# Three 32 KB-row buffers in place of four 16 KB-row buffers, and a pipeline of four stages in place of five, in a graph attention kernel

## The chip, the cores and the metric

The kernel runs on one core of one Trainium2 chip. The metric is the device time of one execution in microseconds; three executions of the kernel before took 718.99, 719.43 and 722.22 us, with a median of 719.43 us. The core has a matrix engine (PE, whose weight loads are listed as PEld), a vector engine (DVE), a scalar engine (ACT), a general engine (POOL) and a queue engine (SP) that issues transfers. Sixteen DMA engines carry the transfers of all queues.

## The reference

One layer of graph attention over 8192 nodes with 128 features, a residual sum and a layer norm:

```python
h = x @ W
e = (h @ a1)[:, None] + (h @ a2)[None, :]
e = where(e > 0, e, 0.2 * e)
e = where(adj > 0, e, NEG)          # adj: 8192 x 8192 int32, 1 with probability 0.000244
out = layernorm(x + elu(softmax(e, axis=1) @ h))
```

The adjacency matrix is 268.4 MB and holds about two ones in a row. A row without any has equal weights on all 8192 nodes, which gives the mean of x.

## The kernel before

The matrix is read once, and the few ones of each row are found on the way. 128 rows are a *tile* (64 tiles); a tile is loaded in two *halves* of 4096 columns (128 partitions by 16 KB, 2 MB). Two tiles are a *group*, so there are 32 groups, with four halves (quarters q = 0 to 3 of `step`) in each. Each half is used twice:

- PE *folds* it (`fold_half`, L649 and L653): nine products sum eight slices of 512 columns, weighted by powers of two, into one PSUM bank, so that a number in the bank tells in which columns of the half the ones stand. DVE takes the eight largest numbers of each row (`pick`, MAX8).
- ACT squares it and sums it (`square_half`, L551), only to count the ones; the count is compared at the end with what was found, and rows in which they differ (none here) would be computed again.

A group's further work runs in stages, one step of the loop later for each. In the step that folds group n, the functions with p1 work on group n-1, p2 on n-2, and so on:

- `lists` (DVE, at the end of a group's own step) turns the picked numbers into column codes and counts them.
- p1: `count_starts` (PE) sums the counts over the rows, `route` (DVE) and `fill_edges` (PE) bring the ones of a group into one list of 640 edges, `indices` (DVE) makes row numbers of x, `gather` (POOL) fetches these rows of x with five indirect DMAs, and `edges_to_rows` and `mark_empty` (POOL) build masks.
- p2: `neighbour_scores` (DVE), `send_scores` (PE), `scores` (DVE), `exp_weights` (ACT), `weights` (DVE), `send_shares` (PE), `edge_weights` (DVE), `spread_weights` (POOL).
- p3: `sum_neighbours` (PE), `copy_sums` (ACT), `times_W` (PE), `exp_elu` (ACT).
- p4: `finish` (DVE: the sum with x, and the statistics of the norm) and `norm_factors` (POOL); p5: `scale` (ACT).

Every engine runs its own list, written by hand in its `step`, in the order in which the calls stand. Engines wait for one another by counting semaphores. What sets the pace of the loads is `adj_sb` with LOAD_SLOTS = 4 places of one half: SP waits until the half that lay in a place is squared and folded, and then issues the next load into it. All loads, those of x (four, behind the first four halves) and the stores of the result stand in SP's one queue; the gathers go through POOL's queue, and W and a through ACT's.

The first six steps are written out, the middle ones are a loop with two steps in its body, and the last two and what is left of the last groups (the *tail*, from the landing of the last half on) are written out again. In the tail, five matrix products in a row and the like (`keep_warm`) do no work. SP stores groups 0 to 11 and 12 to 23 of the result in one transfer each as soon as it has issued the last load, and the others as they are ready.

## Time and profile before

| | |
|---|---|
| median of three runs | 719.43 us |
| profiled execution | 721.3 us |
| its span, first to last instruction | 719.5 us |
| granted PE clock, mean | 0.882 |
| busy: PE, DVE, ACT, POOL | 557.4, 480.7, 520.5, 443.6 us |
| DMA packets, bytes | 34582, 285.57 MB |

The profiled execution took 1.8 us more than its span (721.3 against 719.5 us). The views are: the page, whose strips cut the span in 40 slices of 18 us; the table by stretches, with the busy time of each engine, the granted clock (1.00 is 2.4 GHz, 0.50 is 1.2 GHz), the DMA engines' mean busy share and what they moved; the chain of waits; and the timeline, in which a row gives start, duration, engine, line, operation, output and input, and in brackets how long the engine had been idle and what ended that.

### The profile page before, as it was taken

The numbers are of one execution on the slowest core, as the hardware profiler recorded it, in microseconds if no ns is written. First come the engines' busy times: TensorE is split into PE (matmuls) and PEld (weight loads), VectorE is DVE, ScalarE is ACT, GpSimd is POOL, SyncE is SP. The second block draws the span as 40 slices with busy tenths as digits, with TensorE's granted clock in tenths as the row PEclk, the third lists the DMA queues.
The fourth block names the chain that finished last, engine by engine and source line by source line (L and its number), as shares of the span: only waits on it lengthen the run. The fifth ranks groups of instructions, "written<-read, shape, count | busy, mean of one in ns | idle before, by whom it ended". The sixth has DMA issues, their size and how long they took to land.

```text
span 719.5 us, 11920 instructions
## 1 busy us (share of the span) xinstructions
PE 557.4 (77%) x3071; PEld 351.2 (49%) x3071; DVE 480.7 (67%) x2051; ACT 520.5 (72%) x414; POOL 443.6 (62%) x668
## 2 busy tenths in 40 slices
PE   0858799987778887778888787887778787777884
PEld 0323455554455554555455554554455554544583
DVE  1474777767766667667667667677766667667565
ACT  0847578787878777887878787878878777878511
POOL 2016267766766676676667676667666766777741
PEclk9987798899999999998889999799999999999957
DMA  9999999999999999999999999999999999999901
GB/s 353 326 422 422 384 413 429 427 422 425 428 425 429 426 426 429 425 427 425 428 426 427 427 428 427 428 426 426 428 425 428 429 427 428 426 423 424 284 17 31
DMA packets 34582, 285.57 MB, mean 397 GB/s; under 512 B 5512, under 2 KB 13856, under 8 KB 18048
## 3 DMA queue, kind: packets, MB, share of 16 engines
q1 hardware_dynamic: 29008, 276.83, 92.1%
q0 software_dynamic: 5120, 8.42, 3.3%
q8 instruction: 9, 0.15, 0.1%
q10 hardware_dynamic: 432, 0.07, 0.1%
q14 instruction: 13, 0.11, 0.0%
HBM read 283.18 MB, written 4.19 MB: 399 GB/s over the span
## 4 chain that ended last, share of the span: by engine, by line
DMA 63%; PE 12%; ACT 10%; DVE 6%; issue 5%; POOL 2%; SPq 0%; ACTq 0%; POOLq 0%; DVEq 0%
DMA adj_sb<-in_adj 60%; ACT adj_squared L551 10%; PE fold L653 7%; DMA a_sb<-in_L_gnn_a 2%; PE misc L678 2%; PE fold L649 1%; POOL edge_row L362 1%; PE x_att_ps L701 1%; DMA nb<-in_x,index 1%; DVE s_all L838 1%; PE small L668 1%; DVE x_times_wa L836 1%; DVE top_map L852 0%; DVE spread L374 0%; POOL nb L497 0%
## 5 line engine op out<-in xcount | busy, mean ns | idle before, releaser
L551 ACT ACTIVATE adj_squared<-adj_sb 128x4096 bf16<-128x4096 int32 x128 | 462.4, 3613 | 103.2 <-DMA adj_sb<-in_adj 97.2
L653 PE MATMUL fold<-adj_sb,bit_ident 128*128 128x512 bf16 x1024 | 302.0, 445 | 0.0
L497 POOL DMA_INDIRECT nb<-in_x,index x160 | 165.7, 1036 | 92.4 <-issue 64.2
L653 PEld LDWEIGHTS fold<-adj_sb,bit_ident 128*128 128x128 bf16 x1024 | 109.4, 107 | 150.6 <-issue 61.0
L649 PE MATMUL fold<-col_no,ident_bf 128*128 128x512 bf16 x128 | 53.2, 416 | 114.2 <-DMA adj_sb<-in_adj 101.7
L852 DVE MAX8 top_map<-fold 128x8 f32<-128x512 f32 x128 | 89.5, 699 | 67.1 <-PE fold L653 62.4
L362 POOL TENSOR_SCALAR edge_row<-row_iota,edge_in 128x128 f32<-128x128 int32 x186 | 129.4, 710 | 0.0
L378 POOL TENSOR_TENSOR spread<-edge_row,edge_w 128x384 f32<-128x384 f32 x60 | 51.9, 885 | 66.4 <-DVE edge_w L965 66.3
L477 POOL TENSOR_SCALAR empty_diag<-ident,counts 128x128 f32<-128x128 f32 x64 | 42.2, 665 | 68.5 <-DVE counts L889 35.4
L649 PEld LDWEIGHTS fold<-col_no,ident_bf 128*128 128x128 bf16 x128 | 16.4, 128 | 129.1 <-issue 101.4
L701 PEld LDWEIGHTS x_att_ps<-spread,nb 128*128 128x128 f32 x372 | 58.6, 225 | 9.8 <-issue 4.7
L701 PE MATMUL x_att_ps<-spread,nb 128*128 128x128 f32 x372 | 60.4, 306 | 1.0 <-DVE spread L374 1.0
L913 DVE COPY edge_in<-small 128x90 f32<-128x90 f32 x32 | 8.0, 252 | 74.4 <-PE small L668 74.4
L678 PE MATMUL misc<-t_slot,edge_row 128*128 128x10 f32 x384 | 51.0, 267 | 4.5 <-DVE t_slot L934 2.8
L678 PEld LDWEIGHTS misc<-t_slot,edge_row 128*128 128x128 f32 x384 | 49.0, 204 | 4.9 <-issue 3.0
L668 PE MATMUL small<-sent,row_edge 128*128 128x18 f32 (+1 forms) x384 | 43.1, 250 | 6.0 <-DVE row_edge L902 5.9
L668 PEld LDWEIGHTS small<-sent,row_edge 128*128 128x128 f32 (+1 forms) x384 | 40.7, 175 | 10.0 <-DVE row_edge L902 8.0
L687 PE MATMUL small<-share,row_edge 128*128 128x10 f32 (+1 forms) x384 | 41.8, 241 | 0.5 <-DVE share L956 0.5
L687 PEld LDWEIGHTS small<-share,row_edge 128*128 128x128 f32 (+1 forms) x384 | 40.9, 176 | 2.7 <-DVE share L956 1.1
L930 DVE CUSTOM_DVE_ANT_0 dot<-nb,wa_bc 128x128 f32<-128x128 f32 x160 | 40.2, 306 | 2.7 <-DMA nb<-in_x,index 2.7
L556 ACT ACTIVATE weight<-score_e 128x20 f32<-128x20 f32 x32 | 7.0, 219 | 45.6 <-DVE score_e L948 45.6
L902 DVE SCALAR_TENSOR_TENSOR row_edge<-edge_no,sent,below_end 128x320 f32<-128x320 f32 x64 | 35.8, 600 | 1.1
(120 smaller groups left out, 623.4 us busy)
## 6 DMA issues: line engine op xcount, KB each, us to landing
adj_sb<-in_adj SPq DMA_DIRECT2D x127, 2048.0 KB, 15.9
out<-x_sb SPq DMA_DIRECT2D x2, 1536.0 KB
nb<-in_x,index POOLq DMA_INDIRECT x160
adj_sb<-in_adj SPq DMA_DIRECT2D x2, 1024.0 KB, 15.1
out<-x_sb SPq DMA_DIRECT2D x5, 128.0 KB
out<-x_sb SPq DMA_DIRECT2D x1, 384.0 KB
W_sb<-in_L_gnn_W ACTq DMA_DIRECT2D x1, 64.0 KB, 7.9
x_sb<-in_x SPq DMA_DIRECT2D x4, 0.5 KB, 17.7
```

Source lines behind the costliest of these rows:

```text
L362: last_one = eng.tensor_scalar(edge_row[:, g, t, k, :], row_iota[:, t * P:(t + 1) * P], edge_in[:, c, ROW_COL:ROW_COL + 1], None, ALU.is_e ...
L378: last_one = eng.tensor_tensor(spread[:, t, :, :], edge_row[:, g, t, :, :], mine.unsqueeze(2).to_broadcast([P, SPAN, P]), ALU.mult)
L477: last = nc.gpsimd.tensor_scalar(empty_diag[:, g, t, :], ident[:], found[:, t:t + 1], None, ALU.is_gt)
L497: nc.gpsimd.indirect_dma_start(out=nb_of(j, g)[:, c, :], out_offset=None, in_=x[:, :], in_offset=bass.IndirectOffsetOnAxis(ap=index[:, g, ...
L551: nc.scalar.activation(adj_squared[:, h % 2, :], adj_sb[:, h % LOAD_SLOTS, :], ACT.Square, accum_out=half_sum[:, h:h + 1]).then_inc(square ...
L649: nc.tensor.matmul(fold[:, h % LOAD_SLOTS, :], ident_bf[:], col_no[:], start=True, stop=False)
L653: last = nc.tensor.matmul(fold[:, h % LOAD_SLOTS, :], bit_ident[:, b, :], adj_low[:, h % LOAD_SLOTS, b * FOLD:(b + 1) * FOLD, 0], start=Fa ...
L668: last = nc.tensor.matmul(edge_in_ps[lo:hi, c, :], row_edge[:, g, t, e:e + hi - lo], sent[:, t, :], start=True, stop=True)
L678: last = nc.tensor.matmul(t_row_ps[:, t, :], edge_row[:, g, t, k, :], t_slot[:, c, :], start=k == 0, stop=k == SPAN - 1)
L687: last = nc.tensor.matmul(share_ps[lo:hi, c, :], row_edge[:, g, t, e:e + hi - lo], share[:, t, :], start=True, stop=True)
L701: nc.tensor.matmul(x_att_of(j, g)[:, t, 0:P], nb_of(j, g)[:, c, :], spread[:, t, k, :], start=k == 0, stop=False)
L852: nc.vector.max(top_map[:, q, :], fold[:, h % LOAD_SLOTS, :]).then_inc(picked, 1)
```

## The change

Places of 32 KB per partition: `adj_sb` now has three places of one whole tile, and one transfer of 4 MB with rows of 32 KB fills a place. Only the last tile comes in three transfers, of 16, 8 and 8 KB per row. SP waits for the tile that lay in a place: both of its halves squared and folded. PSUM keeps its four banks for the folds (BANKS).

The order in a step: on PE `sum_neighbours` of p3 stands behind the first fold in place of the second, and `times_W` of p3 before the third fold in place of behind the fourth. On ACT `copy_sums` and `exp_elu` of p3 and `exp_weights` of p2 stand before the third square. On DVE `finish` now works on p3, and stands behind `weights`; `edge_weights` stands before `lists` (not in the final step). ACT's `scale` works on p4. The loop's body has six steps in place of two. Buffers with two sets are still alternated (`g % SETS`). In the tail DVE's `indices` of the final group stands before `neighbour_scores` of the one before it, and SP waits for the final gather before it issues any store. `adj_squared` has one place in place of two, and the products of x with W a are made in eight parts in place of four.

```diff
-    GROUPS = 2
+    SETS = 2
+    GROUPS = 6
...
-    LOAD_SLOTS = 4
+    BANKS = 4
+    TILE_SLOTS = 3
+    LOAD_SLOTS = 2 * TILE_SLOTS
...
-        adj_squared = sb("adj_squared", [P, 2, HALF], bf16)
+        adj_squared = sb("adj_squared", [P, HALF], bf16)
...
+                    for t in range(g * PAIR, (g + 1) * PAIR):
+                        if not (first(i) and t < TILE_SLOTS):
+                            sp.wait_ge(squared, i * HALVES + 2 * (t + 1 - TILE_SLOTS))
+                            sp.wait_ge(folded, i * HALVES + 2 * (t + 1 - TILE_SLOTS))
+                        slot = t % TILE_SLOTS
+                        space = adj_sb[:, 2 * slot:2 * slot + 2, :].rearrange("p s c -> p (s c)")
...
+                        if is_last_half(i, 2 * t + 1):
...
+                        else:
+                            nc.sync.dma_start(space, tile).then_inc(loaded[slot], 16)
...
+                sp.wait_ge(gathered[final[1] % SETS], uses(*final) + 16 * CHUNKS)
                 for lo, hi in STORES:
...
ACT step
-                    now, p2, p3, p5 = (stage(i, g, k) for k in (0, 2, 3, 5))
-                    if p5:
-                        scale(*p5)
+                    now, p2, p3, p4 = (stage(i, g, k) for k in (0, 2, 3, 4))
                     square_half(*now, 0)
-                    square_half(*now, 1)
-                    square_half(*now, 2)
                     if p3:
                         copy_sums(*p3)
+                    square_half(*now, 1)
+                    if p4:
+                        scale(*p4)
                     if p2:
                         exp_weights(*p2)
-                    square_half(*now, 3)
                     if p3:
                         exp_elu(*p3)
+                    square_half(*now, 2)
+                    square_half(*now, 3)
...
PE step
                     fold_half(*now, 0)
+                    if p3:
+                        sum_neighbours(*p3)
                     if p1:
                         count_starts(*p1)
                     fold_half(*now, 1)
-                    if p3:
-                        sum_neighbours(*p3)
                     if p1:
                         fill_edges(*p1)
                     if p2:
                         send_scores(*p2)
+                    if p3:
+                        times_W(*p3)
                     fold_half(*now, 2)
                     fold_half(*now, 3)
-                    if p3:
-                        times_W(*p3)
...
DVE step
-                    if p4:
-                        finish(*p4)
+                    pick(*now, 0)
                     if p1:
                         route(*p1)
                     if p2:
                         neighbour_scores(*p2)
-                    pick(*now, 0)
                     if p1:
                         indices(*p1)
                     pick(*now, 1)
                     if p2:
                         scores(*p2)
                         weights(*p2)
+                    if p3:
+                        finish(*p3)
                     pick(*now, 2)
                     pick(*now, 3)
+                    if p2 and not is_final(*now):
+                        edge_weights(*p2)
                     lists(*now)
-                    if p2:
+                    if is_final(*now):
                         edge_weights(*p2)
...
DVE tail
                 route(*final)
+                indices(*final)
                 neighbour_scores(*back1)
-                indices(*final)
                 scores(*back1)
                 weights(*back1)
-                finish(*back3)
                 edge_weights(*back1)
```

On PE, in the last step but the tail, before: `fill_edges` (small), `send_scores` (misc), the third and fourth fold, and then `times_W` (h_ps).

```order
L668 MATMUL small<-sent,row_edge 128x18 x2
L668 MATMUL small<-sent,row_edge 64x18 x2
L668 MATMUL small<-sent,row_edge 128x18 x2
L678 MATMUL misc<-t_slot,edge_row 128x10 x6
L649 MATMUL fold<-col_no,ident_bf 128x512
L653 MATMUL fold<-adj_sb,bit_ident 128x512 x8
L649 MATMUL fold<-col_no,ident_bf 128x512
L653 MATMUL fold<-adj_sb,bit_ident 128x512 x8
L713 MATMUL h_ps<-W_sb,x_att 128x128 x2
```

The same step of the changed kernel, from `count_starts` (misc from counts) on; `sum_neighbours` stands right before these rows.

```order
L675 MATMUL misc<-counts,before 128x2
L663 MATMUL fold<-col_no,ident_bf 128x512
L667 MATMUL fold<-adj_sb,bit_ident 128x512 x8
L682 MATMUL small<-sent,row_edge 128x18 x2
L682 MATMUL small<-sent,row_edge 64x18 x2
L682 MATMUL small<-sent,row_edge 128x18 x2
L692 MATMUL misc<-t_slot,edge_row 128x10 x6
L727 MATMUL h_ps<-W_sb,x_att 128x128 x2
L663 MATMUL fold<-col_no,ident_bf 128x512
L667 MATMUL fold<-adj_sb,bit_ident 128x512 x8
L663 MATMUL fold<-col_no,ident_bf 128x512
L667 MATMUL fold<-adj_sb,bit_ident 128x512 x8
```

`times_W` moved before the third fold, and `count_starts` now stands behind `sum_neighbours`.

On DVE, in the tail of the kernel before: the end of `neighbour_scores` of the group before the final one, then `indices` of the final group (edge_in to index), then `scores`.

```order
L930 ISA dot,t_edge<-nb,wa_bc 128x128
L930 ISA t_edge 128x1
L934 TENSOR_TENSOR t_slot<-at_slot,t_edge 128x50
L913 COPY edge_in<-small 128x90
L915 TENSOR_TENSOR at_slot<-edge_less_slot,edge_in 128x50
L918 TENSOR_TENSOR own_code<-edge_in,at_slot 128x50
L920 TENSOR_REDUCE edge_code<-own_code 128x5
L924 TENSOR_SCALAR index<-edge_code 128x5
L942 TENSOR_TENSOR score<-misc,s_all 128x20
```

The same place of the changed kernel, from the last instruction of `route` on.

```order
L916 SCALAR_TENSOR_TENSOR row_edge<-edge_no,sent,below_end 128x320 x2
L927 COPY edge_in<-small 128x90
L929 TENSOR_TENSOR at_slot<-edge_less_slot,edge_in 128x50
L932 TENSOR_TENSOR own_code<-edge_in,at_slot 128x50
L934 TENSOR_REDUCE edge_code<-own_code 128x5
L938 TENSOR_SCALAR index<-edge_code 128x5
L944 ISA dot,t_edge<-nb,wa_bc 128x128
L944 ISA t_edge 128x1
```

`indices` now stands before `neighbour_scores`, and both behind `route` of the final group.

## Rows read from the trace of the kernel before

**Rows 1.** The page: DMA busy tenths, GB/s, packets, shares of the chain.
```profile
DMA  9999999999999999999999999999999999999901
GB/s 353 326 422 422 384 413 429 427 422 425 428 425 429 426 426 429 425 427 425 428 426 427 427 428 427 428 426 426 428 425 428 429 427 428 426 423 424 284 17 31
DMA packets 34582, 285.57 MB, mean 397 GB/s; under 512 B 5512, under 2 KB 13856, under 8 KB 18048
DMA 63%; PE 12%; ACT 10%; DVE 6%; issue 5%; POOL 2%; SPq 0%; ACTq 0%; POOLq 0%; DVEq 0%
```

**Rows 2.** Table by stretches: engines' busy time, clock, DMA share, GB/s.
```profile
24.00:36.00 12.00, 12.00 (x44) 5.29 (x43) 5.96 (x24) 11.80 (x8) 0.00 (x0) 1.00 1.06 290
...
84.00:92.00 8.00, 8.00 (x34) 3.81 (x34) 3.18 (x12) 6.59 (x4) 4.99 (x5) 0.68 0.81 300
...
108.00:662.00 554.00, 444.60 (x2566) 283.36 (x2565) 387.79 (x1707) 442.98 (x354) 380.98 (x573) 0.90 1.01 427
...
676.00:680.00 4.00, 3.77 (x19) 1.49 (x16) 3.40 (x22) 0.93 (x3) 3.28 (x4) 1.00 1.04 298
```

**Rows 3.** The loads: SP's waits (total, times, longest), issue to landing.
```profile
SPq L392 <- PE fold L653: 459.2, 118, 12.2
...
adj_sb<-in_adj SPq DMA_DIRECT2D x127, 2048.0 KB, 15.9
```

**Rows 4.** The start: the load of a in the chain, SP's issue of x.
```profile
1.67 17.64 DMA a_sb<-in_L_gnn_a
...
2.87 28.17 SPq L403 DMA_DIRECT2D x_sb<-in_x  x4
```

**Rows 5.** Timeline of the third step: DVE's last part of `own_scores`, PE's third fold.
```profile
74.74 2.29 DVE L838 TENSOR_REDUCE s_all<-x_times_wa 128x16 f32<-128x2048 f32 x1
...
84.16 0.59 PE L649 MATMUL fold<-col_no,ident_bf 128*128 128x512 bf16 x1
```

**Rows 6.** Timeline of PE in a step of the loop: a fold behind a wait.
```profile
316.83 0.39 PE L649 MATMUL fold<-col_no,ident_bf 128*128 128x512 bf16 x1 [3.10 <-DMA adj_sb<-in_adj]
317.06 2.92 PE L653 MATMUL fold<-adj_sb,bit_ident 128*128 128x512 bf16 x8
```

**Rows 7.** Timeline of the final step and the tail.
```profile
662.31 3.62 ACT L551 ACTIVATE adj_squared<-adj_sb 128x4096 bf16<-128x4096 int32 x1 [1.57 <-DMA adj_sb<-in_adj]
...
665.96 0.84 PE L701 MATMUL x_att_ps<-spread,nb 128*128 128x128 f32 x6
...
667.21 3.62 ACT L551 ACTIVATE adj_squared<-adj_sb 128x4096 bf16<-128x4096 int32 x1 [1.18 <-DMA adj_sb<-in_adj]
...
667.76 1.29 PE L668 MATMUL small<-sent,row_edge 128*128 128x18 f32 x12
...
670.24 0.38 PE L649 MATMUL fold<-col_no,ident_bf 128*128 128x512 bf16 x1
...
672.26 0.38 PE L649 MATMUL fold<-col_no,ident_bf 128*128 128x512 bf16 x1
...
674.60 0.70 DVE L852 MAX8 top_map<-fold 128x8 f32<-128x512 f32 x1 [1.04 <-PE fold L653]
...
678.50 0.17 DVE L889 TENSOR_REDUCE counts<-is_code 128x2 f32<-128x20 f32 x1
...
681.40 1.40 PE L668 MATMUL small<-sent,row_edge 128*128 128x18 f32 x12 [1.14 <-DVE row_edge L902]
...
684.00 0.29 DVE L930 CUSTOM_DVE_ANT_0 dot<-nb,wa_bc 128x128 f32<-128x128 f32 x1 [2.66 <-DMA nb<-in_x,index]
...
685.31 0.24 DVE L913 COPY edge_in<-small 128x90 f32<-128x90 f32 x1
...
686.32 0.17 DVE L924 TENSOR_SCALAR index<-edge_code 128x5 uint32<-128x5 f32 x1
...
690.17 0.28 DVE L971 TENSOR_SCALAR z_one<-z_exp 128x256 f32<-128x256 f32 x1
...
691.92 0.25 DVE L984 BATCH_NORM_AGGREGATE mean_var<-stats 128x2 f32<-128x6 f32 x2
...
696.90 0.28 DVE L930 CUSTOM_DVE_ANT_0 dot<-nb,wa_bc 128x128 f32<-128x128 f32 x1
```

239 lines of the change are left out of this document (120 added, 119 removed).

## The prediction

> **What bounds the kernel now.** I read the page's strips first. The DMA strip stands at 9 in all slices up to 684 us, and the GB/s strip lies between 422 and 429 from slice 7 on (two slices late in the run apart) [rows 1]. The table by stretches says the same in one row: 427 GB/s at a DMA share of 1.01 from 108 to 662 us, while PE, the busiest engine, is busy 444.6 of 554 us [rows 2]. The chain of waits puts 63% on DMA [rows 1]. Then I looked at whether this is a full queue or a wait for places: SP waits 459.2 us in 118 waits for a fold to free a place, but a load of 2 MB lands 15.9 us after its issue [rows 3]. At 427 GB/s 2 MB take 4.9 us, so three loads are always under way. The DMA engines, not the places, set the pace. The time has three parts: the start up to about 108 us, in which the strip shows weak slices (353, 326, 384, 413 GB/s), the plateau, and the tail behind the last landing. The halves of the last group wake ACT at 662.31 and 667.21 us, 4.9 us apart [rows 7]; so the last bytes land at about T = 672.1 us, and the tail is 719.5 - 672.1 = 47.4 us.
>
> **Longer rows on the plateau.** The change leaves the bytes and halves the number of packets of the matrix, from 16384 of 16 KB to 8192 of 32 KB. What a packet costs besides its bytes can be read from a stretch with small ones: from 676 to 680 us the stores of x_sb run in rows of 512 B at 298 GB/s [rows 2]; the page counts 8344 packets between 512 B and 2 KB, the stores' 8192 among them [rows 1]. On one of 16 engines a 512 B packet then takes 16 x 512 B / 298 GB/s = 27.5 ns, and a 16 KB packet at 427 GB/s 16 x 16384 / 427 = 613.9 ns. The difference, 586.4 ns for 15872 B, is 27.1 B per ns, and leaves 27.5 - 18.9 = 8.6 ns of fixed cost in each packet. Saved are 8192 packets x 8.6 ns / 16 engines = 4.4 us. The stretch of x, from 24 to 36 us with 290 GB/s, would give 9.3 ns and 4.8 us. The other end is nothing, if these costs hide behind long packets. I take 4.4 us since two stretches agree, and keep 0 and 4.8 for the range.
>
> The Trainium skill speaks against this term: its page "DMA: Bandwidth & Descriptors" (Rules for kernel authors) asks for 128 partitions and at least 1 MiB in a transfer for full bandwidth, and both kernels have that. The same page (Why small descriptors are slow) gives a fixed 3 cycles per packet beside one for each 32 B, and calls joining packets worthwhile only up to 256 B; as an estimate from that page, 3 of 515 cycles would become 3 of 1027, and the sum would gain some 1.9 us here in place of 4.4. The measured 27.5 ns of a 512 B packet are above what those cycles alone explain.
>
> **The start.** The load of a lands 17.64 us after its issue though it is 512 B, since it shares the engines with the first 8 MB of the matrix [rows 4]. Behind 32 KB packets its packets wait twice as long, so I expect the landing at about 24 us, when the first 8 MB are through. The Trainium skill has this as a rule ("DMA: Bandwidth & Descriptors", Queues, rings and completion order): an engine takes turns between queues packet by packet. The delay of about 5 us costs nothing: SP is held by the issue of x from 2.87 to 31.04 us in both kernels [rows 4], and the first two tiles are squared and folded before the DMA engines are through with x and the third tile. Should the cover go, it would cost up to 5 us.
>
> Between 84 and 92 us the DMA engines ran dry: share 0.81, 300 GB/s [rows 2]. That is (427 - 300) x 8 / 427 = 2.4 us lost. The reason is the work on x: DVE is in `own_scores` until 77.03, `route` comes behind it, and PE's third fold of that step starts only at 84.16 [rows 5], so a place comes free too late. Three whole tiles hold 4 MB more, which is 9.8 us of DMA time, and this dip goes. But in the next steps a place waits for both of its halves, and on ACT the third square now waits for `exp_weights`, with the scores of p2 and both first folds ahead of it. By my chain the tile of the sixth step is issued about when the one before it has landed, for a new dip of 0 to 4 us; I take 1.7. The start's balance is -0.7 us (from -2.4 to +1.6).
>
> **The plateau's order.** A step takes about 20.3 us by DMA: 285.57 MB [rows 1] without x and the result (4.19 MB each) is 8.66 MB for each of 32 groups, at 427 GB/s [rows 2]. The longest loop through the engines in the new order is: `send_shares`, `edge_weights`, `lists`, `count_starts`, `route`, `neighbour_scores`, `send_scores`, `times_W`, two folds. From [rows 7]: a fold is 672.26 - 670.24 = 2.0 us, `lists` with its pick 678.67 - 674.60 = 4.1, `route` 681.40 - 678.67 = 2.7 with the count, `neighbour_scores` 685.3 - 684.0 = 1.3, `fill_edges` and `send_scores` 670.24 - 667.76 = 2.5. With about 2.5 us for the three small pieces that is 17 us. Behind a wait of 3 us PE runs a stretch at the low clock (the fold behind the 3.10 us wait takes 2.92 us for its eight products [rows 6]), once a step at 0.90 mean clock [rows 2]; that adds 1.7 us. At 19 us the loop still fits under 20.3, or 20.1 with the packets' gain, and costs nothing. The gathers' packets wait longer, but have 8 us until they are wanted. The larger loop body costs nothing either while DMA sets the pace.
>
> **The tail.** Here the change loses. Before, the final group's halves arrive one by one, 4.9 us apart. Now its first tile arrives whole, at L = T' - 9.8 us (T' being the new last landing), where before the second half came. PE does: fold 2.0, `sum_neighbours` 1.8 (665.96 to 667.76), count 0.3, and DVE `route` 2.3 and `neighbour_scores` 1.4, to L + 8.1; then `send_scores` 1.4, `times_W` 0.5 and two folds 4.0, to L + 14.1. On DVE `indices` 1.2 (685.31 to 686.49), a pick 0.7, `scores` and `weights` about 2.2 and `finish` 2.0 (690.17 to 692.17) lie before the last two picks, which end at L + 15.6 = T' + 5.8. Before, the last pick ended at 675.3, or T + 3.2 [rows 7]. That is 2.6 us later. With one low-clock stretch behind the wait for the tile it is 4.3. Next `indices` of the final group moves before `neighbour_scores` of the one before. That started at 684.00 = T + 11.9, when its gather landed; now it starts behind route, fill and indices: 678.67 to 681.40 to 682.8, then 1.2 more, so T + 6.5 + 4.2 + 1.2 = T + 11.9 in the old times, and so T' + 14.5 to T' + 16.2 with the delay. All behind it keeps its order. The final gather comes earlier by the swap, but DVE reached its rows only at 696.90, without a wait [rows 7], so this is worth nothing; `finish` leaves the tail for nothing as well, since DVE waited there for PE. The stores now start behind the final gather, at about T' + 25, and need 3.5 MB / 298 GB/s = 12 us, to T' + 37, before the late groups are ready at about T' + 43. I take +3.5 us for the tail (bounds 0, if the clock is kinder, and +6.5 with two more low stretches).
>
> **The sum.** -4.4 - 0.7 + 3.5 = -1.6 us. The profiled execution took 721.3 us (719.5 and 1.8 around it), which gives 719.7; the runs' median is 1.9 us under the profiled one, so I predict 717.8 us.
>
> **Rivals.**
> 1. *The DMA gains more and the tail pays less.* 4.8 us of packets, the whole dip of 2.4 gained, the tail at +1 or +2: -5.5 us, 714. For it: the plateau is pure DMA. Against it: the tail's arithmetic.
> 2. *The packets' cost is hidden.* Then 0 - 0.7 + 3.5 = +2.8 us, 722.2. For it: the plateau's DMA share is 1.01 [rows 2], so packets overlap, and a fixed cost in one may lie beside the bytes of another. Against it: two stretches of small packets that agree. The Trainium skill's rule on 1 MiB, above, points the same way.
> 3. *The engines become the bound* (slower). Place: the loop of a step, through `exp_weights` before the third square and `lists` behind `edge_weights`. It decides from the point where that loop passes 20.1 us, which needs one low-clock stretch more in each step, 1.7 us over my 19. At 0.4 us a step over 28 steps it costs 11 us: 729.
> 4. *The change does not do what it says*: rows of 32 KB are cut into the packets of before, or move slower. The first gives rival 2's time; the second, at 1% of 640 us, gives 6 us more, 728.
>
> **Chances.** About 0.5%, or 3.6 us, is what a measurement tells from no change. Forecast 0.42, rival 1 0.28, rival 2 0.16 (a quarter of it over the 0.5%), rival 3 0.10, rival 4 0.04. Of the forecast's own range, 714.5 to 721.5, a little falls below 715.8. Faster 0.32, same 0.46, slower 0.22. The range is 713.0 to 724.0: it leaves out part of rival 3 and of a larger gain.
>
> **What would show it.** Packets: some 8190 fewer than 34582, and the plateau at 429 to 431 GB/s; 427 is rival 2. Start: no weak slice at 84 to 92 us, a small one near 100 to 120. Plateau: PE waits for adj_sb, once a step and longer, and DMA stays at 9; if SP's loads land 10 us after issue in place of 20 or more, rival 3 holds. Tail: the last pick 6 to 7.5 us behind the last landing, and about 51 us from there to the end. The forecast is wrong if the plateau's rate moves by over 1%, or the tail stays at 47 us.

## The result, and the profile after

| | before | after |
|---|---|---|
| median, us | 720.46 (718.99 to 722.22) | 748.37 (746.46 to 753.54) |
| profiled span, us | 719.5 | 751.7 |
| granted PE clock, mean | 0.882 | 0.844 |

The change makes the kernel slower: ratio 1.0398, 95% interval 1.0335 to 1.0460. I had predicted 717.8 us in a range of 713 to 724. One of the twelve runs of before_new_order, below, was a slow one of 1672.45 us, and its time here is the median of the other eleven.

The page of the kernel after: the clock and GB/s strips (40 slices of 18.8 us), the packets, and the chain by engine, which answer to [rows 1].

```profile
PEclk9998799889899796899888688888868888998857
...
GB/s 375 326 417 432 422 378 428 420 417 426 423 418 425 422 420 421 333 406 431 412 426 432 403 337 399 421 419 403 423 367 352 411 428 418 422 428 313 14 121 120
DMA packets 25536, 285.79 MB, mean 380 GB/s; under 512 B 4505, under 2 KB 12849, under 8 KB 17041
...
DMA 29%; PE 28%; DVE 23%; issue 12%; POOL 7%; POOLq 0%; DVEq 0%; ACTq 0%; ACT 0%; SPq 0%
```

There are 9046 packets fewer (34582 - 25536), and the best slices stand at 431 and 432 GB/s, above anything before. But slices of 333, 337, 352 and 367 lie between them, and DMA's share of the chain falls from 63% to 29%. The table by stretches (columns as in [rows 2]) shows the dip of before filled, and the plateau lower:

```profile
84.00:92.00 8.00, 7.78 (x33) 5.16 (x33) 3.81 (x15) 3.26 (x2) 3.88 (x4) 0.59 1.00 430
...
108.00:690.00 582.00, 489.78 (x2546) 307.45 (x2591) 416.13 (x1704) 445.94 (x358) 376.90 (x574) 0.84 0.98 409
```

SP's waits in after, and then the landings of loads and gathers; they answer to [rows 3]:

```profile
SPq L399 <- PE fold L667: 493.6, 60, 17.2
```
```profile
adj_sb<-in_adj SPq DMA_DIRECT2D x63, 4096.0 KB, 18.4
...
nb<-in_x,index POOLq DMA_INDIRECT x160, 8.6
```

A load of 4 MB needs 9.8 us of DMA and lands 18.4 us after its issue, so less than two are under way, where before three of 2 MB were. The chain of waits of after, in order of time (start, us, what), shows what took the place of DMA:

```profile
384.17 11.05 DMA nb<-in_x,index
400.29 3.62 PE fold L667 x8
412.64 5.48 issue
421.29 2.36 PE small L682 x12
431.37 12.18 DMA nb<-in_x,index
...
542.54 6.25 issue
```

It runs through the gathers' landings (nb), and twice here through a stop in which DVE waits for nothing that the profile knows ("issue"). On DVE's timeline such a stop lies between `lists` of one round of the loop and the first pick of the next:

```profile
412.48 0.16 DVE L903 TENSOR_REDUCE counts<-is_code 128x2 f32<-128x20 f32 x1
418.51 0.70 DVE L866 MAX8 top_map<-fold 128x8 f32<-128x512 f32 x1 [5.87 <-issue]
```

The stops at 412.6 and 542.5 us are 129.9 us apart, six steps; the third of them stands in the chain at 284.02 us. The table of DVE's waits (total, times, longest) counts all three, and DVE's waits for a gather:

```profile
DVE dot L944 <- DMA nb<-in_x,index: 22.7, 14, 3.1
DVE top_map L866 <- issue: 18.7, 3, 6.6
```

The rate does not fall during a stop but 10 us and more behind it. That is what one expects if the loads already issued land first. The stretches before and after 430 us:

```profile
420.00:430.00 10.00, 8.71 (x35) 6.62 (x36) 6.79 (x32) 2.59 (x3) 3.38 (x4) 0.50 0.99 424
430.00:440.00 10.00, 8.67 (x48) 5.10 (x47) 6.86 (x27) 9.69 (x8) 6.58 (x10) 0.91 0.64 235
```

Against 427 GB/s this one dip loses (427 - 235) x 10 / 427 = 4.5 us.

At the end: the first square of the final group, the last fold but one, and the last pick; these answer to [rows 7].

```profile
688.93 3.62 ACT L563 ACTIVATE adj_squared<-adj_sb 128x4096 bf16<-128x4096 int32 x1
...
700.40 3.62 PE L667 MATMUL fold<-adj_sb,bit_ident 128*128 128x512 bf16 x8
...
706.69 0.70 DVE L866 MAX8 top_map<-fold 128x8 f32<-128x512 f32 x1 [1.82 <-PE fold L667]
```

The last pick starts at 706.69 us in place of 674.60 [rows 7], 32.1 us later. From there to the end both kernels need the same: 751.7 - 706.69 = 45.0, and 719.5 - 674.60 = 44.9 us. So everything was lost ahead of the last pick. The packets of the two traces divide it: the last packet of the matrix ends at 695.4 us in place of 671.6, and the rest of the run behind it takes 56.3 us in place of 47.9.

### The profile page after: what moved, and what is told of

It reads as the page before. It is cut to its first block, busy times and chain, and to the rows that moved or that the text cites. A ratio compares the mean times of both kernels' runs of the same rounds, so it can differ in the third digit from the quotient of the medians.

```text
span 751.7 us, 11407 instructions
## 1 busy us (share of the span) xinstructions
PE 596.6 (79%) x3018; PEld 374.1 (50%) x3071; DVE 511.8 (68%) x2059; ACT 518.9 (69%) x414; POOL 434.8 (58%) x668
## 2 busy tenths in 40 slices
DMA packets 25536, 285.79 MB, mean 380 GB/s; under 512 B 4505, under 2 KB 12849, under 8 KB 17041
## 4 chain that ended last, share of the span: by engine, by line
DMA 29%; PE 28%; DVE 23%; issue 12%; POOL 7%; POOLq 0%; DVEq 0%; ACTq 0%; ACT 0%; SPq 0%
DMA nb<-in_x,index 23%; PE fold L667 12%; POOL nb L507 6%; PE misc L692 5%; PE small L682 3%; DMA adj_sb<-in_adj 3%; DMA a_sb<-in_L_gnn_a 3%; DVE dot L944 3%; PE small L701 3%; PE h_ps L727 2%; DVE from_base L876 2%; DVE row_edge L916 2%; DVE below_end L912 1%; PE fold L663 1%; DVE lead L879 1%
## 5 line engine op out<-in xcount | busy, mean ns | idle before, releaser
L667 PE MATMUL fold<-adj_sb,bit_ident 128*128 128x512 bf16 x1003 | 297.6, 442 | 7.8 <-DMA adj_sb<-in_adj 2.9
L369 POOL TENSOR_SCALAR edge_row<-row_iota,edge_in 128x128 f32<-128x128 int32 x186 | 108.8, 596 | 0.2 <-DVE edge_in L927 0.2
L692 PE MATMUL misc<-t_slot,edge_row 128*128 128x10 f32 x384 | 67.2, 312 | 28.5 <-DVE t_slot L948 27.7
L692 PEld LDWEIGHTS misc<-t_slot,edge_row 128*128 128x128 f32 x384 | 65.3, 262 | 30.4 <-issue 30.3
L682 PE MATMUL small<-sent,row_edge 128*128 128x18 f32 (+1 forms) x384 | 48.8, 267 | 38.5 <-DVE row_edge L916 38.3
L715 PEld LDWEIGHTS x_att_ps<-spread,nb 128*128 128x128 f32 x372 | 49.8, 204 | 32.4 <-POOL spread L385 23.6
L944 DVE CUSTOM_DVE_ANT_0 dot<-nb,wa_bc 128x128 f32<-128x128 f32 x160 | 37.9, 294 | 22.8 <-DMA nb<-in_x,index 22.7
L663 PE MATMUL fold<-col_no,ident_bf 128*128 128x512 bf16 x98 | 46.3, 472 | 2.9 <-DMA adj_sb<-in_adj 2.9
L727 PE MATMUL h_ps<-W_sb,x_att 128*128 128x128 f32 x120 | 33.8, 433 | 0.0
L916 DVE SCALAR_TENSOR_TENSOR row_edge<-edge_no,sent,below_end 128x320 f32<-128x320 f32 x64 | 32.6, 551 | 1.1
L499 POOL COPY counts_all<-counts 128x4 f32 (+1 forms) x32 | 6.4, 200 | 43.4 <-DVE row_edge L916 43.4
## 6 DMA issues: line engine op xcount, KB each, us to landing
adj_sb<-in_adj SPq DMA_DIRECT2D x63, 4096.0 KB, 18.4
```

The costliest lines, as they stand in the source:

```text
L369: last_one = eng.tensor_scalar(edge_row[:, g % SETS, t, k, :], row_iota[:, t * P:(t + 1) * P], edge_in[:, c, ROW_COL:ROW_COL + 1], None, A ...
L663: nc.tensor.matmul(fold[:, h % BANKS, :], ident_bf[:], col_no[:], start=True, stop=False)
L667: last = nc.tensor.matmul(fold[:, h % BANKS, :], bit_ident[:, b, :], adj_low[:, h % LOAD_SLOTS, b * FOLD:(b + 1) * FOLD, 0], start=False, ...
L682: last = nc.tensor.matmul(edge_in_ps[lo:hi, c, :], row_edge[:, g % SETS, t, e:e + hi - lo], sent[:, t, :], start=True, stop=True)
L692: last = nc.tensor.matmul(t_row_ps[:, t, :], edge_row[:, g % SETS, t, k, :], t_slot[:, c, :], start=k == 0, stop=k == SPAN - 1)
L715: nc.tensor.matmul(x_att_of(j, g)[:, t, 0:P], nb_of(j, g)[:, c, :], spread[:, t, k, :], start=k == 0, stop=False)
```

## The experiments

All are timed in three or five rounds against the kernel before. "Body" is the number of steps in the loop's body. The kernel before had medians of 720.07 to 721.03 us beside all of them but three: beside after_body3_ring_cut, after_body3_halves_tail and after_body3_ring_tail, which were timed together, it took 723.97 us. Between these three and the others the ratio compares better than the time.

| kernel | body | places and rows | order | us | ratio and interval |
|---|---|---|---|---|---|
| after_unrolled | none | 3 tiles, 32 KB | new | 739.95 | 1.0264 [1.0232, 1.0296] |
| after_16k_rows | 6 | 3 tiles, 16 KB | new | 753.65 | 1.0450 [1.0414, 1.0486] |
| before_body6 | 6 | 4 halves | old | 743.29 | 1.0305 [1.0268, 1.0342] |
| old_order_32k | 6 | 3 tiles, 32 KB | old | 756.06 | 1.0469 [1.0429, 1.0509] |
| after_body3 | 3 | 3 tiles, 32 KB | new | 732.52 | 1.0166 [1.0149, 1.0183] |
| before_body4 | 4 | 4 halves | old | 751.11 | 1.0419 [1.0400, 1.0439] |
| before_unrolled | none | 4 halves | old | 734.95 | 1.0191 [1.0173, 1.0209] |
| old_order_32k_body3 | 3 | 3 tiles, 32 KB | old | 740.17 | 1.0271 [1.0249, 1.0293] |
| before_new_order | 2 | 4 halves | new | 723.03 | 1.0028 [1.0009, 1.0046] |
| after_body3_indices_first | 3 | 3 tiles, 32 KB | new, changed | 804.76 | 1.1156 [1.1138, 1.1174] |
| after_body3_16k_rows | 3 | 3 tiles, 16 KB | new | 735.42 | 1.0196 [1.0180, 1.0212] |
| after_body3_ring_cut | 3 | 3 tiles, 32 KB | new, changed | 736.65 | 1.0188 [1.0154, 1.0222] |
| after_body3_halves_tail | 3 | 3 tiles, 32 KB | new | 732.24 | 1.0119 [1.0073, 1.0165] |
| after_body3_ring_tail | 3 | both edits | new, changed | 732.27 | 1.0139 [1.0099, 1.0178] |
| after_body3_half_places | 3 | 6 halves, 16 KB | new | 731.30 | 1.0129 [1.0108, 1.0150] |
| half_places_four_of_six | 3 | 4 of 6 halves | new | 735.60 | 1.0216 [1.0179, 1.0253] |
| half_places_nb_first | 3 | 6 halves | new | 729.37 | 1.0130 [1.0090, 1.0169] |
| before_large_buffer | 2 | 4 of 6 halves | old | 721.59 | 1.0015 [0.9998, 1.0032] |

### The loop's body

**before_body6** is the kernel before with six steps in the body and nothing else changed:

```diff
-            with eng.Fori(3, BODIES - 1) as i:
-                for g in range(GROUPS):
-                    step(i, g)
+            with eng.Fori(1, (BODIES - 1) // 3) as third:
+                for b in range(3):
+                    for g in range(GROUPS):
+                        step(third * 3 + b, g)
```

> The kernel before with a loop body of six steps in place of two (four rounds in place of twelve); the same steps in the same order. Theory A: the body is fetched again in each round, with a stop at each jump; with 4 places of 2 MB, behind 16 KB packets, each costs 2 to 6 us of DMA time, so 728 to 745 us. Theory B: nothing changes, 718 to 722 us.

It costs 23 us by itself: 743.29 us. DVE stops behind the loop's jumps as in after, here at the first instruction of `finish`; two rows of its timeline:

```profile
280.00 0.29 DVE L972 TENSOR_SCALAR z_one<-z_exp 128x256 f32<-128x256 f32 x1 [5.73 <-issue]
...
409.70 0.29 DVE L972 TENSOR_SCALAR z_one<-z_exp 128x256 f32<-128x256 f32 x1 [5.75 <-issue]
```

What is different from before is seen in the queues that carry code ("instruction": packets, MB, share). From 230 to 640 us the kernel before has no row of them at all; before_body6 has these two:

```profile
q14 instruction: 19, 0.16, 0.1%
q8 instruction: 1, 0.02, 0.0%
```

and after in the same stretch:

```profile
q14 instruction: 21, 0.17, 0.1%
q8 instruction: 2, 0.03, 0.0%
```

So a body of two steps stays in the engines, and part of one of six is fetched again in every round. The Trainium skill has this as a rule, and I had not weighed it ("Runtime: NRT & Kernel Launch", Instruction fetch mechanics): an engine holds only a small window of code, filled in order, and a taken branch to a target outside it waits for a fetch. The trace agrees, and gives 5.7 to 6.6 us for one such stop on DVE, in before_body6 and after.

**before_body4** puts four steps in the body of before, in the same way. 

> The kernel before with four steps in the loop body in place of two (six rounds of four); nothing else. With six steps it took 743.3 us against 720.6. Theory A says that there is a size from which the body is fetched again in each round: if four steps lie under it, 719 to 722 us and no code transfers between 180 and 640 us; if over it, stops on DVE behind six jumps, and 740 us or more.

It took 751.11 us, with shorter rounds and so more stops: five jumps back in place of three. One row of DVE's waits, which holds these five of 6.2 to 6.7 us and a small one (a second group holds the picks):

```profile
DVE z_one L972 <- issue: 32.2, 6, 6.7
```

**after_unrolled** and **before_unrolled** write all steps out, without a loop.

> The changed kernel with all 30 steps written out in place of a loop with six steps in its body; nothing else. Theory A (the large loop body no longer stays in the engines' instruction stores and is fetched again from memory in each round, with a stop of some 6 us on DVE at each jump back): the four jumps at 284, 412, 542 and 670 us cost about 6 to 8 us each, so the time falls from 748 to 720 to 730 us. Theory B (the gathers land 10 us behind their last issue in place of 5.5, behind packets of 32 KB, and this closes a loop through indices, gather and neighbour_scores): no jump is involved, and the time stays within 5 us of 748.

> The kernel before with all steps written out, so that no engine jumps back. If what costs is the jump back into code that must be fetched again, the stops of 5.5 us on DVE are gone and the time is 719 to 726 us, though code is fetched all along. If it is the fetching itself (its share of the DMA engines, or late code in straight lines), the time is like that with six steps in the body, 735 to 745 us.

739.95 us, 8 less than after, and 734.95 us, 14 more than before; I had expected 720 to 730 and, had only the jumps cost, 719 to 726. No jump is left, but now all code comes in once, during the run (230 to 640 us, before_unrolled):

```profile
q8 instruction: 14, 0.23, 0.2%
q14 instruction: 21, 0.17, 0.1%
```

What this costs is seen in no single stop. DVE's longest wait between 200 and 640 us for nothing that the profile knows is 2.9 us in before_unrolled. Its waits for PE are somewhat longer, but they stand in the kernel before as well; first before, then before_unrolled:

```profile
DVE edge_in L913 <- PE small L668: 74.4, 27, 4.9
```
```profile
DVE edge_in L910 <- PE small L665: 94.6, 28, 5.9
```

and ahead of such a wait PE itself waits for a tile:

```profile
466.67 0.61 PE L646 MATMUL fold<-col_no,ident_bf 128*128 128x512 bf16 x1 [4.10 <-DMA adj_sb<-in_adj]
...
474.42 0.25 DVE L910 COPY edge_in<-small 128x90 f32<-128x90 f32 x1 [5.87 <-PE small L665]
```

The plateau of before_unrolled stands at 420 GB/s in place of 427 (200 to 640 us). That late code is what lowers it is likely, since nothing else was changed, but which engine it holds up is not shown. The same page of the Trainium skill calls the fetch of straight code mostly hidden and unrolling the better choice; here the loop of two steps beats the unrolled kernel by 14 us. The measurement decides.

**after_body3** gives the changed kernel three steps in its body, with three sets of buffers (SETS = 3), since three places and two sets only meet every six steps. Small buffers of the end and of the start share space to make room.

```diff
-    SETS = 2
-    GROUPS = 6
+    SETS = 3
+    GROUPS = 3
```

> The changed kernel with three steps in the loop body in place of six (eight rounds behind six steps that are written out; the alternating buffers have three sets in place of two, which also loosens waits on them; x times W a is made in sixteen parts, and scratch of the repair code shares room). Places, 32 KB rows, waits and orders as changed. Theory A (the loop body): if three steps stay in the engines' stores as two did, no stop of 5.5 to 6 us on DVE follows a jump, and the time falls by 15 to 25 us, to 723 to 733; what is then left over 720 is the new order's. If three steps are too many as well, there are eight stops, and the time rises to 755 or more. Theory B (32 KB packets in front of the gathers): nothing of this, 745 to 750.

732.52 us: 15.9 us of the 28 are gone. The number of sets and the small buffers changed along with the body here; that the body alone costs this much is shown by before_body6, where nothing else was changed. From 230 to 640 us no row of an instruction queue is left, and no stop of over 1.3 us on DVE. The plateau (200 to 640 us) is

```profile
200.00:640.00 440.00, 375.95 (x2010) 237.59 (x2046) 330.65 (x1349) 349.35 (x282) 299.41 (x458) 0.87 1.00 424
```

### Packets and the gathers' landing

**after_16k_rows** splits each tile's load into two of 16 KB rows, with the same places and waits; **after_body3_16k_rows** does so in after_body3:

```diff
-                            nc.sync.dma_start(space, tile).then_inc(loaded[slot], 16)
+                            nc.sync.dma_start(space[:, 0:HALF], tile[:, 0:HALF]).then_inc(loaded[slot], 16)
+                            nc.sync.dma_start(space[:, HALF:N], tile[:, HALF:N]).then_inc(loaded[slot], 16)
```

> The changed kernel with each tile loaded in two transfers with rows of 16 KB (the same three places of one tile, the same waits, the same orders, the last tile's first half in two transfers too). Theory B: the gathers land 5 to 6 us behind their last issue again, the steps between two jumps fall from 20.5 to 20.3 us or less, and 8 to 15 us come back: 733 to 740. Theory A alone: the packets of the code's fetches wait less, so a stop at a jump shrinks from 6 to some 3 us, 10 us come back at most, and the gathers' latency makes no difference in the steps between the jumps. No effect at all (748 and above) would leave the orders as the cause.

> The changed kernel with three steps in its body and each tile in two transfers of 16 KB rows (same places, same waits). If the landing of the gather behind 32 KB packets costs time once the stops at the jumps are gone, this is faster than 732.5 us although it gives the packets' gain back: 727 to 731 us, with the gather landing 4.7 to 5.2 us behind its issue. If the packets' gain of 4.4 us is real and the gather costs nothing, 736 to 738 us. With six steps in the body the same edit cost 5.3 us.

They are slower by 5.3 and 2.9 us, or by their ratios 3.7 and 2.2 us, with intervals that overlap. In the traces of the pair with three steps the last packet of the matrix ends at 681.4 us in place of 676.7. So the gain of the larger loads is real, but its size is known only as 2 to 5 us; rows and transfers were halved together. In both the gathers land early, and DVE no longer waits for them (in after it waited 22.7 us in 14 waits). So a gather that lands late costs less than the longer rows gain.

**after_body3_indices_first**: in after_body3 the chain of waits goes from gather to gather, at a period of 20.3 us:

```profile
379.92 11.30 DMA nb<-in_x,index
400.29 11.29 DMA nb<-in_x,index
```

Measured on the packets, from the start of a gather's last issue to the end of its last packet, a landing takes 10.8 us in after_body3 and 5.7 us in before (medians, 200 to 640 us); in before no gather of this stretch is in the chain. `neighbour_scores` starts when the gather lands, `indices` stands behind it, and the next gather behind that: a ring. The experiment swaps the two calls in DVE's step.

> The changed kernel with three steps in its body, and indices of p1 before neighbour_scores of p2 in DVE's step, so that the next gather is issued without waiting for the landing of the last. In the kernel with three steps in the body the gather lands 9.8 us behind its last issue and neighbour_scores starts 0.5 us behind the landing in nearly every step. If this ring (gather, neighbour_scores, indices, gather) sets the 20.4 us step there, the landing gets slack, the step falls to 20.1 us, the last landing to 668 to 671 us, and the time to 723 to 728 us. If DMA sets the step, nothing moves: 731 to 734 us. If DVE's order as a whole is the ring, it gets slower, by one indices call of 1.2 us in the way of the scores.

804.76 us: the ring is cut, but the other one, from `lists` through `route`, `indices`, `neighbour_scores` and `send_scores` to the third fold, grows past the DMA's time. Two rows of PE and DMA (its waits, 200 to 640 us; the plateau):

```profile
PE misc L692 <- DVE t_slot L948: 56.4, 20, 3.0
```
```profile
200.00:640.00 440.00, 350.84 (x1810) 223.67 (x1810) 289.88 (x1196) 308.11 (x249) 264.74 (x405) 0.83 0.92 379
```

At 379 GB/s a step of 8.66 MB takes 22.8 us. One swapped pair costs 72 us, which argues, without showing it, that in the changed kernel the loop through the engines is within a microsecond or so of DMA's 20.3.

**after_body3_ring_cut** therefore also moves `send_scores` behind the third fold:

```diff
-                    if p2:
-                        send_scores(*p2)
                     if p3:
                         times_W(*p3)
                     fold_half(*now, 2)
+                    if p2:
+                        send_scores(*p2)
                     fold_half(*now, 3)
```

(ACT: `exp_weights` and `exp_elu` behind the third square; DVE: `indices` ahead of `neighbour_scores`.)

> The changed kernel with three steps in its body; on DVE indices of p1 ahead of neighbour_scores of p2, on PE times_W before the third fold and send_scores behind it, on ACT exp_weights and exp_elu between the third and the fourth square. The ring through the gather's landing is cut, and send_scores no longer holds up the third fold. If that ring is what sets 20.4 us a step, the step becomes what DMA gives, 20.1 us: the last landing at 669 to 673 us and the time 725 to 731 us. In the kernel with indices ahead alone, the step was 22.7 us, because send_scores ran before the third fold behind indices and neighbour_scores; by its rows this order should take 19.7 us. If the order is still longer than DMA (another ring), the last landing comes at 680 us or later. If instead DMA itself gives only 424 GB/s with whole tiles in three places, the last landing stays at 676 to 677 us.

Now PE waits for tiles, as before the change (its waits from 200 to 640 us, and the plateau from 200 to 420 us):

```profile
PE fold L663 <- DMA adj_sb<-in_adj: 45.7, 24, 3.5
```
```profile
200.00:420.00 220.00, 185.09 (x997) 115.51 (x1013) 159.25 (x659) 173.21 (x140) 142.64 (x222) 0.85 1.00 424
```

and the rate is the same 424 GB/s. So the ring through the gather was in step with DMA, not what held it back; my ring theory falls. The whole took 736.65 us, 4 us more than after_body3 by the time and 1.6 us by the ratio. In the traces the last packet of the matrix ends at 676.7 us in both kernels, so what was lost was lost in the tail.

### The orders

**old_order_32k** and **old_order_32k_body3** have the old order and five stages with the new loads:

> The changed kernel with the orders of the kernel before on PE, ACT and DVE (five stages, indices of the final group behind neighbour_scores in the tail), but three places of 32 KB rows, the loop body of six steps and SP's wait before the stores as changed. If the new orders are to blame for the plateau, the time falls to 725 or less. Theories A and B, which lie in the body and the packets, both say that most of the loss stays: 738 to 748 us, the rest being the tail (3 to 8 us).

> Three places of 32 KB rows with the engines' orders of the kernel before, and the same loop of three steps and three buffer sets as in the run after_body3. With the loop of six steps the old order took 756.1 us against 748.4 of the new one. Theory A: if three steps stay resident, both lose 15 to 25 us. If the new order is what makes three whole-tile places workable, the old order stays 4 to 10 us behind the new one here too. Theory B (gathers that land 10 us behind their last issue): the old order has its indices behind pick 0 and neighbour_scores as the new one, and would be as slow as before, 750 to 756.

756.06 and 740.17 us, 7.7 us more than the new order with the same body, or 5.1 and 7.6 us by the ratios. **before_new_order** has the new order, four stages, and all else of before.

> The kernel before (halves of 16 KB rows, four places, a loop body of two steps) with the new order of calls alone: sum_neighbours, times_W, copy_sums, exp_elu, finish and edge_weights where the changed kernel has them, four stages in place of five, and in the tail indices before neighbour_scores. If the loop body explains the loss and the orders fit under the 20.3 us that the DMA takes for a step, as my prediction has it, the plateau stays at 427 GB/s, the last landing at 672 (+-1) us, and the time is 718 to 723 us. If the new order itself is part of the loss (its loop through the engines is longer than 20.3 us), the last landing comes 3 us later or more and the time is 725 us or more.

723.03 us, a ratio of 1.0028 [1.0009, 1.0046], and the plateau stands at 427:

```profile
200.00:640.00 440.00, 373.87 (x2029) 232.65 (x2029) 328.73 (x1333) 350.71 (x284) 299.16 (x450) 0.88 1.01 427
```

The new order by itself costs some 2 us (0.6 to 3.3 by the interval), with the plateau's rate as before; it earns 5 to 8 us where places are whole tiles.

### The tail

**after_body3_halves_tail** loads the last tile but one in two transfers with a wait for each:

```diff
+                        elif is_late_half(i, 2 * t + 1):
+                            nc.sync.dma_start(space[:, 0:HALF], tile[:, 0:HALF]).then_inc(loaded[slot], 16)
+                            nc.sync.dma_start(space[:, HALF:N], tile[:, HALF:N]).then_inc(half_loaded, 16)
```

> The changed kernel with three steps in its body, and the last tile but one in two transfers, one per half, each with its own wait. If the whole tile's late arrival is the 2.6 to 4.3 us of my tail term, the tail shrinks from 53.6 us to 49 to 51 us and the time from 732.5 to 728 to 730 us. If the tail is longer for other reasons (the low clock, the chain from the last pick on), nothing moves: 731.5 to 733.5 us.

> Both edits together. If each is worth what its own theory says and they add, 721 to 728 us; with the packets' gain of 4.4 us then fully seen and a tail as before, it would come within 1% of the kernel before. If neither holds, 732 us.

732.24 us. By the ratio, 1.0119 against 1.0166, that is some 3 us less, with intervals that overlap; the trace shows nothing won. PE starts the first fold of the final group at 667.92 us without a wait for the tile, as in after_body3 at 668.28, and the last pick stays where it was, at 685.34 us where after_body3 has 685.68: the engines are behind at that point. Both edits together took 732.27 us, where 721 to 728 was expected. **after_body3_half_places** is the kernel with three steps in the body and six places of one half, each with its own transfer of 16 KB rows, its own wait and release:

```diff
-                    for t in range(g * PAIR, (g + 1) * PAIR):
-                        if not (first(i) and t < TILE_SLOTS):
-                            sp.wait_ge(squared, i * HALVES + 2 * (t + 1 - TILE_SLOTS))
+                    for h in range(g * 2 * PAIR, (g + 1) * 2 * PAIR):
+                        if not (first(i) and h < LOAD_SLOTS):
+                            sp.wait_ge(squared, i * HALVES + (h + 1 - LOAD_SLOTS))
```

> The changed kernel with three steps in its body, but with six places of one half: 16 KB rows, one transfer, one wait and one release for each half, as in the kernel before. Against after_body3_16k_rows only the grouping of two halves is undone. If whole-tile places are what lowers the rate (421 and 424 GB/s) and lengthens the tail, the plateau is back at 427 GB/s, the last landing at 669 to 673 us, the tail at 45 to 49 us as in before_new_order, and the time 715 to 722 us: no slower than the kernel before, perhaps a little faster, since six places fill the dip at 84 to 92 us. If the three-step body or the larger buffer lowers the rate, the plateau stays at 421 GB/s and the time is 730 us or more. The packets' gain of 3 to 5 us is not in this kernel by either theory.

731.30 us: 4.1 us less than after_body3_16k_rows, which differs only in whole tiles. The last pick moves from 689.16 to 682.02 us, though 2.3 of these 7.1 us are lost again between there and the end:

```profile
682.02 0.70 DVE L864 MAX8 top_map<-fold 128x8 f32<-128x512 f32 x1 [1.05 <-PE fold L665]
```

So a place of a whole tile costs some 4 us here. But the rate did not come back as I expected (200 to 420 us):

```profile
200.00:420.00 220.00, 189.18 (x989) 118.52 (x1006) 163.86 (x668) 175.07 (x141) 146.44 (x226) 0.84 1.01 420
```

### The rate of the plateau

Where the 420 come from is seen in short stretches. In after_body3_16k_rows the first and third row cover a gather, the others do not:

```profile
316.00:324.00 8.00, 5.96 (x31) 3.63 (x30) 6.16 (x24) 7.94 (x5) 6.58 (x10) 0.87 1.01 410
324.00:336.00 12.00, 11.60 (x65) 7.57 (x64) 8.75 (x39) 8.05 (x10) 6.50 (x12) 0.80 1.00 427
336.00:344.00 8.00, 5.76 (x30) 3.16 (x29) 5.96 (x23) 7.62 (x5) 6.56 (x10) 0.90 1.01 409
```

and in before_new_order, with the same order and rows, so do the first and third:

```profile
310.00:318.00 8.00, 7.07 (x45) 4.52 (x43) 5.58 (x21) 8.00 (x5) 5.92 (x9) 1.00 1.01 426
318.00:329.00 11.00, 8.58 (x52) 5.24 (x53) 9.31 (x40) 7.65 (x10) 7.83 (x14) 1.00 1.01 429
329.00:337.00 8.00, 5.96 (x28) 3.05 (x27) 5.57 (x22) 8.00 (x5) 5.92 (x9) 0.79 1.01 421
```

While a gather runs, all transfers together move 409 to 410 GB/s in the one and 421 to 426 in the other; over all gathers from 200 to 640 us the packets give 410 and 425 GB/s. Three runs looked for the reason. The first uses four of the six half places, the second puts `nb` at an address ahead of the matrix buffer, the third gives the kernel before the large buffer alone:

> after_body3_half_places with the same buffer of six half places at the same addresses, of which only four are used, so that as many loads are under way as in the kernel before. If the depth of the queue lowers the rate while a gather runs, the plateau is back at 427 GB/s and the time is 720 to 725 us (as before_new_order, with its dip at 84 to 92 us). If the addresses or the body of three steps do it, the plateau stays at 420 to 422 GB/s and the time is 729 to 735 us.

> after_body3_half_places with nb, the gathers' target, at a lower address than the six half places in place of behind them; six places in use. If it is the address of the gathers' target that lowers the rate, 427 GB/s and 716 to 724 us. If it is the depth of the queue, nothing moves: 729 to 733 us.

> The kernel before with adj_sb allocated for six halves, of which only the first four are used, and with adj_squared in one place and the products of x with W a in eight parts, which makes room for it. Order, stages, body and loads are those of the kernel before. If the addresses of what lies behind the matrix buffer lower the rate while a gather runs, the plateau falls to 420 to 422 GB/s, with 409 to 412 in the stretches with a gather, the last landing comes at 679 to 683 us and the time is 727 to 732 us. If they do not, the plateau stays at 427 GB/s and the time at 719 to 723 us; the three sets or the three-step body remain as the cause.

735.60, 729.37 and 721.59 us; plateaus of 421, 421 and 427 GB/s. The last, from 200 to 640 us:

```profile
200.00:640.00 440.00, 353.42 (x2045) 225.71 (x2043) 307.64 (x1350) 353.54 (x284) 301.49 (x454) 0.90 1.01 427
```

So it is neither the depth of the queue, nor the address of the gathers' target alone, nor the large buffer alone. Nor does it need three sets or the three-step body: after_16k_rows has two sets and six steps, and in a stretch that covers a gather, far from a stop, it is as slow. before_body6, with six steps too but the places and order of before, is not, here ahead of its first dip. First after_16k_rows, then before_body6:

```profile
341.00:349.00 8.00, 6.41 (x33) 3.34 (x32) 5.25 (x17) 7.23 (x5) 4.79 (x7) 0.92 1.02 411
```
```profile
270.00:278.00 8.00, 5.23 (x25) 2.90 (x24) 3.82 (x22) 6.00 (x7) 6.18 (x9) 0.79 1.01 424
```

The new order together with the large buffer was not tried apart from the rest, and the cause stays open.

## Why the prediction was wrong

**The failed step** is a clause: "The larger loop body costs nothing either while DMA sets the pace." It costs 23 us in the kernel before (before_body6), and taking it down to three steps wins 15.9 of the 28 us back. I had put it at nothing because DMA set the pace. DMA hides an engine's stop only as long as places are full: a stop of 5.9 to 6.6 us in after holds up picks, then folds, then the place that the next load wants, and behind it the strip drops to 333 to 367 GB/s. The plateau's rate fell from 427 to 409 GB/s, which the prediction had named as a sign of being wrong. None of my rivals had this mechanism; rival 3 had its sign (the engines become the bound) and 729 us, for another cause.

**Packets, -4.4 us: right in kind and about in size.** 16 KB rows in the same places cost 5.3 us with a body of six and 2.9 us with three, 3.7 and 2.2 us by the ratios; the bounds were 0 and 4.8. The cost of 8.6 ns in each packet was not measured apart. The estimate of 1.9 us from the Trainium skill ("DMA: Bandwidth & Descriptors", Why small descriptors are slow) is a little below all four figures. Its rule that 1 MiB in a transfer is enough for full bandwidth ("DMA: Bandwidth & Descriptors", Rules for kernel authors), which rival 2 leaned on, doesn't hold to the last half percent or so here: both kernels are above it, and the larger loads still gain.

**The start, -0.7 us: right in kind.** The load of a landed 23.13 us after its issue; I had said about 24 us. SP was held by x to the same time:

```profile
1.67 23.13 DMA a_sb<-in_L_gnn_a
```
```profile
1.82 28.93 SPq L412 DMA_DIRECT2D x_sb<-in_x  x4
```

The stretch from 84 to 92 us runs at 430 GB/s, and the new dip that I put at 100 to 120 us is in the strip's sixth slice, 378 GB/s (94 to 113 us). It costs (424 - 378) x 18.8 / 424 = 2.0 us, where I had taken 1.7. In the packets of the traces 40 MB of the matrix have landed at 116.4 us before and at 115.6 us after, near the 0.7 us of the forecast.

**The plateau's order, 19 us: probably sized too low, with no consequence that the runs show.** before_new_order shows that the order fits under DMA with half places. In after_body3, with whole tiles, next to nothing is left: PE waits there for a tile four times in the whole run, two of them in this row, and DMA still gives only 424 GB/s:

```profile
PE fold L667 <- DMA adj_sb<-in_adj: 4.7, 2, 3.9
```

That the two go at the same pace does not say which one leads, and ring_cut shows that it was DMA.

**"The gathers' packets wait longer, but have 8 us until they are wanted": wrong as read, without a price that shows.** A landing takes 10.8 us in after_body3 in place of 5.7, and neighbour_scores waits for it in 18 of 32 steps. I had counted the slack of the old order, in which `finish` and other work stood ahead of `neighbour_scores`. But splitting the rows, which brings the landing forward, makes the kernel slower, and cutting the ring leaves the rate as it was.

**A term that was missing:** the rate while a gather runs. I expected 429 to 431 GB/s; after_body3 has 424. The matrix and the gathers are 276.8 MB (268.4 and 8.4), so 424 in place of 430 is 276800 x (1/424 - 1/430) = 9.1 us. Its cause is open.

**The tail, +3.5 us (0 to 6.5): too small, inside its bounds only by luck, and for another reason than mine.** From the end of the matrix's last packet to the end of the run before takes 47.9 us, after_body3 53.5 and after 56.3: 5.6 us more without the stops at the jumps, inside the bounds, and 8.4 us more in the changed kernel itself, outside them. My reason was that the final group's first tile arrives whole. But in after_body3 PE comes to this tile without a wait for it, and after_body3_halves_tail, which brings its first half early, leaves the last pick where it was. The engines come late into the tail. Half places in the whole run, against whole tiles with the same rows, win 4.1 us; what of this is release and what is arrival was not separated. (My own terms up to the two folds add up to L + 13.7 and not 14.1 us, which changes nothing.) The low clock adds to it: in after eight products of a fold take 3.62 us (700.40), and 1.97 at the full clock.

**The sum.** Of the 27.9 us between the medians, 15.9 go with the larger body. The traces of before and after_body3 differ by 10.7 us of the other 12.1: the matrix's last packet ends 5.1 us later, of which the rate makes 276800 x (1/424 - 1/427) = 4.6 us, with the gain of the longer rows already in it, and the tail takes 5.6 us more. The rest, 1.4 us, is not shown apart; what the lower granted clock, 0.844 for 0.882, costs by itself isn't either. No version tried beats the kernel before; closest are before_large_buffer, which leaves all but the buffer as it was, and before_new_order, the change's order alone.

## What to carry to other kernels

A loop's body has a size beyond which its code is fetched again in each round; look for rows of the instruction queues in the middle of the run, and for a stop "<-issue" behind the jump, before lengthening a body to make two periods meet. Larger transfers that gain on the plateau can need larger places, and these have a price of their own: here 2 to 5 us were gained and some 4 us paid. Bringing one late half forward did not win the price back, since the engines were behind by then: look whether anything waits for a transfer before splitting it. When the chain of waits runs through two things at the same period, it doesn't tell which leads: cut one of them.

## What the runs showed of the hardware that was not expected

- A body of two or three steps is not fetched again; four and six steps are, with a stop of 5.7 to 6.7 us on DVE at a jump back. Straight code costs 14 us in place of the loop of two steps, without a stop "<-issue" of more than 2.9 us on DVE between 200 and 640 us (before_unrolled).
- A stop of 6 us on DVE ending at 418.51 us is seen in the loads from 430 to 440 us, at 235 GB/s; one ending at 290.18 us from 300 to 308 us, at 211 GB/s.
- Beside packets of 32 KB a gather's last packet ends 10.8 us after its last issue starts (after_body3), beside packets of 16 KB 5.7 us (before).
- The best slices of the strip reach 431 to 432 GB/s with rows of 32 KB and 427 to 429 with rows of 16 KB, in transfers of 4 and 2 MB.
- A gather lowers the rate beside it to 409 to 410 GB/s in one kernel and 421 to 426 in another with the same rows and order. The packets of 16 KB that start during a gather take 644 ns in after_body3_16k_rows and 617 ns in before_new_order, and 614 to 615 ns outside of gathers in both.
